# First attention of a four-layer graph network: stages of a group two to three blocks closer, boundary blocks weighed on two tiles

## What is computed

```
e     = elu(s_src[src] + s_tgt[tgt])          # alpha 0.2, per edge and head
m     = segment_max(e, tgt)
ex    = exp(e - m[tgt])
denom = segment_sum(ex, tgt)
msg   = ex / denom[tgt] * xp[src]             # xp = x @ W
out   = segment_sum(msg, tgt)
```

## Time and profile before

| what | us |
|---|---|
| median of three runs | 5281.34 |
| lowest and highest | 5273.83, 5284.76 |
| profiled execution: span from first to last instruction | 4482.7 |
| its own total | not given |
| this layer's blocks (first gather to last add) | 1169.1 to 2279.9 |
| PE / DVE / ACT / POOL busy over the span | 3009.7 / 2397.2 / 1262.2 / 3127.6 |

### The profile page before, as it was taken

The page is one execution under the profiler, slowest core; times in us unless marked ns, Lnnn a source line. Parts: engine busy times, 40 slices in busy tenths (PEclk is TensorE's granted clock), DMA queues, the critical chain, the costliest instruction groups (busy, mean ns, idle before and its releaser), DMA issues. The chain is left out here.

```text
span 4482.7 us, 63695 instructions
## 1 busy us (share of the span) xinstructions
PE 3009.7 (67%) x17204; PEld 2319.8 (52%) x17204; DVE 2397.2 (53%) x7686; ACT 1262.2 (28%) x3859; POOL 3127.6 (70%) x3260
## 2 busy tenths in 40 slices
PE   4999999999344544454548888888878344444444
PEld 2555555555234444444448877778874333333333
DVE  6676666655446766676766666666665211111110
ACT  4333333334334544454531111111223000000000
POOL 4777777775477777777427777777760777777776
PEclk8999999999655555555555555555559555555555
DMA  4644444431334444444212223332226422222222
GB/s 98 144 93 94 93 94 93 93 84 27 101 97 108 111 104 106 107 112 103 47 44 61 73 74 79 83 88 61 56 49 239 56 53 53 53 53 53 53 53 62
DMA packets 418284, 370.29 MB, mean 83 GB/s; under 512 B 287216, under 2 KB 321658, under 8 KB 414603
## 3 DMA queue, kind: packets, MB, share of 16 engines
q0 software_dynamic: 103168, 178.48, 17.4%
q1 hardware_dynamic: 311304, 187.65, 15.6%
q10 hardware_dynamic: 3456, 0.01, 0.0%
HBM read 317.35 MB, written 33.83 MB: 78 GB/s over the span
## 5 line engine op out<-in xcount | busy, mean ns | idle before, releaser
L1216 POOL DMA_INDIRECT rel_row<-tab,words_in x806 | 760.5, 944 | 364.3 <-issue 244.4
L1216 POOL DMA_INDIRECT mlp_row<-tab,rec_d x806 | 784.0, 973 | 292.5 <-issue 244.8
L1216 POOL DMA_INDIRECT gat_row<-tab,rec_d x806 | 777.9, 965 | 266.6 <-issue 241.7
L1216 POOL DMA_INDIRECT att_row<-tab,rec_d x806 | 784.1, 973 | 255.7 <-issue 242.0
L1657 PE MATMUL rel_ps_acc<-rel_row,rel_hot 128*128 128x128 f32 x1612 | 415.4, 439 | 586.9 <-DMA rel_row<-tab,words_in 566.0
L1657 PEld LDWEIGHTS rel_ps_acc<-rel_row,rel_hot 128*128 128x128 f32 x1612 | 356.5, 326 | 645.6 <-issue 645.6
L1940 PE MATMUL gat_ps_sum<-gat_row,gat_hot 128*128 128x136 f32 x1612 | 405.8, 427 | 278.5 <-DVE gat_row L2011 249.3
L1697 DVE TENSOR_TENSOR rel_hot<-rel_ps_iota,rel_local 128x512 f32<-128x512 f32 (+1 forms) x208 | 138.5, 674 | 794.1 <-PE rel_ps_acc L1657 794.1
L2170 PE MATMUL att_ps_sum<-att_row,att_hot 128*128 128x136 f32 x1612 | 429.9, 446 | 131.1 <-DVE acc L1582 127.0
L1940 PEld LDWEIGHTS gat_ps_sum<-gat_row,gat_hot 128*128 128x128 f32 x1612 | 349.7, 309 | 302.8 <-issue 264.6
L2170 PEld LDWEIGHTS att_ps_sum<-att_row,att_hot 128*128 128x128 f32 x1612 | 368.3, 324 | 199.9 <-DVE acc L1582 194.8
(11 more groups left out here) (282 smaller groups left out, 5290.4 us busy)
## 6 DMA issues: line engine op xcount, KB each, us to landing
mlp_aim<-in_dst SPq DMA_DIRECT2D x195, 256.0 KB, 66.8
gat_aim<-in_dst SPq DMA_DIRECT2D x195, 256.0 KB
tab<-n_stage SPq DMA_DIRECT2D x25, 1024.0 KB
mlp_row<-in_edge_attr SPq DMA_DIRECT2D x390, 64.0 KB
mlp_row<-tab,rec_d POOLq DMA_INDIRECT x806
gat_row<-tab,rec_d POOLq DMA_INDIRECT x806, 2.6
att_row<-tab,rec_d POOLq DMA_INDIRECT x806
rel_row<-tab,words_in POOLq DMA_INDIRECT x806
```

What stands on the lines that cost most here:

```text
L1216: gp.indirect_dma_start(row[b][:, t, :], None, table, bass.IndirectOffsetOnAxis(offsets(order[k], t), axis=0)).then_inc(s_g[b], 16)
```

## The change

The lags of the stages are made smaller, and `message` and `make_hot` touch the real tiles only.

```diff
             def make_hot(k, q, b):
                 act.wait_ge(s_gap, k + 1)
                 ge(act, s_sum, k - 3)
-                act.activation(hot[b % 4][:], gap[b % 2][:], ACT.Relu, scale=-1.0, bias=1.0).then_inc(s_hot, 1)
+                here = tile_slice(k)
+                act.activation(hot[b % 4][:, here], gap[b % 2][:, here], ACT.Relu, scale=-1.0, bias=1.0).then_inc(s_hot, 1)
...
-            pipeline(act, [(24, at_end(begin_extra)), (4, bring_tgt), (23, keep_sum), (18, measure_gap), (19, make_hot),
-                           (8, at_end(bring_local)), (9, at_end(fifth_exp)), (10, at_end(to_lanes)), (13, at_end(weight)),
-                           (25, at_end(fade_exp))])
+            pipeline(act, [(22, at_end(begin_extra)), (4, bring_tgt), (21, keep_sum), (16, measure_gap), (17, make_hot),
+                           (8, at_end(bring_local)), (9, at_end(fifth_exp)), (10, at_end(to_lanes)), (11, at_end(weight)),
+                           (23, at_end(fade_exp))])
...
-            pipeline(pe, [(0, take), (3, at_end(lanes)), (6, at_end(back)), (14, mm_sum)])
+            pipeline(pe, [(0, take), (3, at_end(lanes)), (4, at_end(back)), (12, mm_sum)])
...
             def message(k, q, b):
                 v.wait_ge(s_wgt, 2 * q + side(b) + 1)
-                part = rows[:, b, :, 0:W].rearrange("p t (h f) -> p t h f", h=H)
-                v.tensor_tensor(part, part, wgt[:, :, b % GROUP].unsqueeze(3).broadcast_to([P, TILES, H, f + 1]),
+                here, wide = tile_slice(k), [P, len(real_tiles(k)), H, f + 1]
+                part = rows[:, b, here, 0:W].rearrange("p t (h f) -> p t h f", h=H)
+                v.tensor_tensor(part, part, wgt[:, here, b % GROUP].unsqueeze(3).broadcast_to(wide),
                                 ALU.mult).then_inc(s_msg, 1)
...
-            pipeline(v, [(0, make_hot_t), (3, at_end(add_terms)), (4, at_end(elu)), (6, at_end(tops)),
-                         (8, at_end(subtract)), (16, message), (19, at_end(fades)),
-                         (20, at_end(scale)), (28, add)])
+            pipeline(v, [(0, make_hot_t), (3, at_end(add_terms)), (4, at_end(elu)), (5, at_end(tops)),
+                         (6, at_end(subtract)), (14, message), (16, at_end(fades)),
+                         (17, at_end(scale)), (25, add)])
```

## The result

The changed kernel takes 5360.01 us (median of four runs, 5349.61 to 5370.94) against 5282.84 us for the kernel before (four runs, 5273.83 to 5284.76), a ratio of 1.0144 with an interval of 1.0131 to 1.0157. It is slower by 77 us, where 10 gained were forecast.

A forecast was written before the change was run, and what follows sets the result against it. The prediction took GpSimd's gathers to bound the first attention up to 2146 us, then VectorE. From 5281.34 it took 8.9 us for gathers no longer slowed by the reverse scan and 0.8 for the tail: 5271.6 us, range 5260 to 5285.

The forecast's parts named there:

- What lies around the span, some 799 us, is not touched: Whole kernel: the difference between the 4482.70 us profile span and the 5281.34 us runs lies outside it, unaffected by the change.
- both new waits are hidden by its wait at the gate, of which 4.9 us are left: First attention, full-pace groups: VectorE's new waits cost nothing, since its gate wait covers them with 4.9 us to spare.
- rival C: First attention: VectorE waits longer at scale for ScalarE's exp than the gate has left; 5292 us and up, chance 0.06.
- Up to 2146 us the gathers set the pace, and packing the other engines' stages closer gives nothing directly: First attention until 2146 us: GpSimd's gathers bound each 40.72 us group, so closer stages elsewhere gain nothing directly.
- New waits of 3.0 us at tops and 1.4 us at scale: VectorE, each group: 3.0 us waiting at tops for ScalarE's copy, 1.4 us at scale for ScalarE's exp.
- Without that cover each microsecond of wait would cost 21 us: First attention: if the gate wait did not hide them, each microsecond of new VectorE wait would cost 21 us.
- The collision rule: A gather starting between above 0.04 and 1.03 us after the reverse scan loses about 1.03 us minus its offset.
- The place of the scan, T + 11.10: The reverse scan moves from 14.46 to 11.10 us after the group's first reduce, missing most gathers: 8.9 us gained.
- Rival B's first way: First attention: the moved reverse scan falls on the next gather; 5277 to 5286 us; chance 0.30 including 0.07 for L1999.
- The tail, 0.8 us gained: First attention from 2147 us, paced by VectorE: less work and shorter messages minus new waits leave 0.8 us gained.
- None at L1999: First attention: gathers lose time beside the reverse scan, L1996, but none beside VectorE's instruction at L1999.
- The shorter message: Thirteen boundary blocks halve their VectorE message to about 0.42 us, saving 0.28 us each, 3.6 us in all.

The follow-up runs named there:

- the PSUM scan: Kernel before, with the forward scan writing its result back into PSUM and the reverse scan reading it there: 5280.37 us, ratio 1.0003, on a long chip.
- few gathers: Kernel before and changed kernel, GpSimd gathering only the first tile of each block in the first attention: 4215.61 and 4299.57 us on a short chip.

## Why the prediction was wrong, step by step

- **"What lies around the span, some 799 us, is not touched"**: this is the step that failed. The difference was not around the span. It lay inside the layers of the executions on a long chip, of which no profile was at hand. A time 18% above the profile's span should have been read as a warning that the profile is not of the runs that are to be forecast; every slack taken from it was then in doubt. With it failed **"both new waits are hidden by its wait at the gate, of which 4.9 us are left"**. On a long chip the gate wait of the kernel before is 111.7 us (with the PSUM scan), not 282.3, and 18.2 are left of it; the new waits put off the messages and sums, GpSimd waits 74.0 us more for its slots, and the layer's gathers take 73.5 us more. The prediction should have held the case that the cover is missing, and given it more than rival C's 0.06.
- **"Up to 2146 us the gathers set the pace, and packing the other engines' stages closer gives nothing directly"**: right on a short chip (1.0005), where the gate gave back 88.1 us for 85.5 of new wait; wrong on a long one, where GpSimd waits for sums in every group.
- **New waits of 3.0 us at tops and 1.4 us at scale**: right in place, somewhat large. With few gathers they are 66.2 / 26 = 2.5 us and 21.4 / 23 = 0.9 us, and with all gathers on a short chip 2.6 and 1.0. On the long chip, with TensorE's lateness in them, they are 8.5 and 5.4 us in the median, and the change adds 81 us at tops and 123 at scale, while gate and subtract give back 216.
- **"Without that cover each microsecond of wait would cost 21 us"**: right. A group with few gathers takes 34.54 instead of 30.66 us, 3.88 us; times 21 that is 81 of the 84 us. Applied to the long chip, 21 x 4.4 = 92 us would have given the result's sign and about its size. That would have been in part luck: the waits there are not the forecast ones, and the cost comes as pauses of GpSimd.
- **The collision rule** (a gather that starts 0.05 to 1.03 us behind the scan ends 0.76 us after it): right to some hundredths. On the short chip the 24 gathers near the scan started 0.05 to 0.79 us after it and took 1.92 to 1.18 us: offset and time add up to 1.97, which is 1.21 + 0.76, in every one within 0.01.
- **The place of the scan, T + 11.10**: off by 0.29 us, because the turns ran in part faster than in the group used for the estimate (the last two at 0.27 us, not 0.42). The forecast called two groups of three free; none in the steady part was. Instead of 8.9 us gained, the first to the last gather took 5.5 us more. Rival B's first way, the next gather in the scan's place, is what happened. A group takes 40.97 us on average, not 40.1 to 40.4 (40.69 before).
- **The tail, 0.8 us gained**: from the start of the last gather to the end of the last add it is 75.2 us against 77.4 before on short chips. The tiles alone give 74.7 and the lags alone 77.7, so the gain is that of the shorter messages (3.6 us forecast for them), and the lags leave the tail as it was. For a short chip too the whole sum was off, then: 9.7 us gained forecast, 2.4 lost measured (within the noise of zero), and the collision's 8.9 is the term that failed.
- **"None at L1999"**: drawn from too few rows. The gathers of the earlier trace rows started 0.17 and 0.03 us before L1999, outside the bad offsets. The one that started 0.27 us into it took 1.23 us. The Trainium skill, "SBUF — State Buffer", "SBUF: two separate sides", says that a VectorE instruction with two SBUF inputs keeps a GpSimd operation that reads SBUF from the shared port pair for its duration. By that rule both instructions slow a gather, if a gather counts as such an operation; the 24 rows at L1997 (1.18 to 1.92 us) and the one that bears on L1999 (1.23 us) agree. It cost nothing in the change, where no gather started there.
- **The gate wait left over, 4.9 us**: 6.68 in the group shown, on a short chip.
- **The shorter message**: 0.42 us forecast, 0.419 measured (13 times); ScalarE's relu 0.405 instead of 0.619. Alone they give 0.9992 (0.9983 to 1.0002), at most some 4 us.
- **Rival C** named the right sign and the right kind of cause (new waits beyond the gate's slack). Its point, "from 0.5 us beyond 4.9 us a group", was passed in two ways on the long chip: the slack was not there, and the waits (8.5 and 5.4 us) were larger.

## What to carry to other kernels

Smaller lags take work out from in front of an engine's waits, and in no run here did they gain time. On short chips they put some 85 us of wait into VectorE's stream, which cost next to nothing under the gathers and 84 us without them. On long chips they cost 77 to 88 us. So judge a closer schedule with its cover taken away (fewer gathers, in one run), and compare the time of the runs with the span of the profile first: where they differ by more than the page's own few microseconds, get the profile of such a run before reading slack from it.

## What the runs showed of the hardware that was not expected

- Chips of one type differ by 18% in this kernel at nearly the same granted clock (the kernel before 0.66 on short chips and 0.67 to 0.68 on long ones, the changed one 0.66 to 0.67 on both) and busy times within 3%. Of the five chips that the experiments fell on two were long in every run, three short. One of the short ones was met three times, each long one once. That the time belongs to the chip, and not to that set of runs, is likely but not shown. The chips of the first profile and of the result are told by their times alone.
- On the long ones, the end of TensorE's work becomes known late, mostly by 3 to 9 us, as long as the layer has gathers, and within 0.02 us after the last of them. In the last layer TensorE's own records are odd there as well, 0.70 us or a multiple apart for over 20 us, and then 36 matmuls in a row, which begin as GpSimd's next gather does after a pause of 5.7 us:

```profile
4617.41 0.37 PE L1657 MATMUL rel_ps_acc<-rel_row,rel_hot 128*128 128x128 f32 x1 [2.43 <-issue]
4620.21 0.37 PE L1657 MATMUL rel_ps_acc<-rel_row,rel_hot 128*128 128x128 f32 x1 [2.43 <-issue]
...
4624.44 5.69 PE L1657 MATMUL rel_ps_acc<-rel_row,rel_hot 128*128 128x128 f32 x36 [0.36 <-issue]
```

- The reverse scan with one input in PSUM did not slow the two gathers that started inside it (0.95 and 0.94 us, where two SBUF inputs made 1.2 to 1.9). These are two cases only, but the forward scan, with one input in PSUM from the start, slowed none of the 24 that started inside it.
